# One Trainium2 core, a quantised decoder layer: x2's bias sums, integers and projections moved to other places

## The reference

```python
x = _layernorm(x + self_attention(x))                # q, k, v with bias, softmax, wo, bo
x = _layernorm(x + cross_attention(context, x))      # keys and values from the context
x = _layernorm(x + ffn(x))

def _qlinear(x, W, b):
    xq, sx, zx = _affine_quantize(x)                 # scale from max(x) - min(x) over the whole tensor
    wq, sw = _sym_quantize(W)
    return jnp.einsum('bsh,oh->bso', xq - zx, wq) * (sx * sw) + b
h = gelu(_qlinear(x, W1, b1)); out = _qlinear(h, W2, b2)      # 128 -> 512 -> 128
```

## Time and profile before

| | us |
|---|---|
| median of 3 runs | 332.87 (332.35 to 334.61) |
| the profiled execution, time | 331.59 |
| its span | 329.9 |
| busy: PE, DVE, ACT, POOL | 269.5, 299.9, 248.1, 238.6 |
| row maxima on DVE, 128 of them | 156.2 busy, 9.5 idle before them |
| last row maximum ends | 244.3 |
| last root of x2 ends | 258.1 |
| extremes of h end | 300.8 |
| last normalisation ends | 326.7 |

### The profile page before, as it was taken

One profiled execution on the slowest core, in us unless ns is written; L12 is line 12 of the kernel. 1 busy time (PEld: TensorE's weight loads), 2 busy tenths in 40 slices (PEclk: granted clock), 3 DMA queues, 4 the chain that ended last, 5 costly groups with the idle time before them and its releaser, 6 DMA issues.

```text
span 329.9 us, 12489 instructions
## 1 busy us (share of the span) xinstructions
PE 269.5 (82%) x4927; PEld 168.4 (51%) x4927; DVE 299.9 (91%) x695; ACT 248.1 (75%) x502; POOL 238.6 (72%) x477
## 2 busy tenths in 40 slices
PE   4677987999999999999999988898887655536991
PEld 3455654666656566665656655555554212112561
DVE  5668799899999999999999999999988779987994
ACT  2237776989988888888888878788775399912995
POOL 2866787897677878687786887776559228998394
PEclk9999999999999999999999999999999897557797
DMA  2353324143342423334243234322100000000025
GB/s 65 111 152 92 108 76 129 52 125 92 107 122 64 123 67 115 84 99 125 69 123 92 79 97 131 90 78 61 52 5 0 3 0 0 1 0 0 2 79 177
DMA packets 48993, 25.14 MB, mean 76 GB/s; under 512 B 6440, under 2 KB 48808, under 8 KB 48936
## 3 DMA queue, kind: packets, MB, share of 16 engines
q1 hardware_dynamic: 46072, 23.55, 24.6%
q10 hardware_dynamic: 2864, 0.80, 1.0%
HBM read 9.39 MB, written 2.10 MB: 35 GB/s over the span
## 4 chain that ended last, share of the span: by engine, by line
POOL 36%; DVE 29%; issue 13%; PE 10%; ACT 5%; SPq 3%; DMA 2%; POOLq 1%; DVEq 0%; ACTq 0%
DVE neg_max L1044 15%; POOL rstd L640 5%; SPq L472 3%; POOL arena_h L670 3%; POOL var_eps L633 2%; ACT arena_h L903 2%; DMA arena_h<-parts_sk 2%; POOL parts_cq L439 2%; POOL parts_ck L439 2%; PE ps L1298 2%; POOL parts_cq L437 2%; POOL parts_ck L437 2%; POOL x_bias L659 2%; DVE o_stats L1206 1%; POOL parts_sq L439 1%
## 5 line engine op out<-in xcount | busy, mean ns | idle before, releaser
L1044 DVE TENSOR_REDUCE neg_max<-ps 128x8 f32<-128x1024 f32 x128 | 156.2, 1220 | 9.5 <-PE ps L1298 9.3
L852 ACT ACTIVATE probs<-ps 128x1024 f32<-128x1024 f32 x64 | 65.5, 1024 | 21.8 <-PE ps L1305 21.8
L843 ACT ACTIVATE probs<-ps 128x1024 f32<-128x1024 f32 x64 | 65.6, 1025 | 15.7 <-PE ps L1305 11.8
L1298 PE MATMUL ps<-arena_h 31*128 31x128 f16 x1024 | 52.3, 220 | 20.4 <-DVE neg_max L1044 11.2
L1298 PEld LDWEIGHTS ps<-arena_h 31*128 31x128 f16 x1024 | 30.5, 94 | 54.9 <-DVE neg_max L1044 38.4
L1305 PE MATMUL ps<-arena_h 32*128 32x128 f16 x1024 | 51.2, 217 | 0.9 <-ACT probs L852 0.9
L1326 PE MATMUL ps<-probs,arena_q 128*32 128x128 f32 x1024 | 41.2, 279 | 1.4 <-ACT u_sb L868 1.4
L1326 PE MATMUL ps<-probs,arena_h 128*32 128x128 f32 x1024 | 41.3, 279 | 0.0
L633 POOL TENSOR_TENSOR var_eps<-mean_var,eps_col 128x1 f32<-128x1 f32 x64 | 12.3, 192 | 38.1 <-DVE mean_var L1026 38.1
L640 POOL TENSOR_TENSOR rstd<-var_eps,minus_half 128x1 f32<-128x1 f32 x64 | 35.3, 551 | 4.7
L1305 PEld LDWEIGHTS ps<-arena_h 32*128 32x128 f16 x1024 | 29.2, 92 | 2.0 <-ACT probs L852 1.5
(11 more groups left out here) (182 smaller groups left out, 657.7 us busy)
## 6 DMA issues: line engine op xcount, KB each, us to landing
arena_h<-parts_sq SPq DMA_DIRECT2D x48, 64.0 KB, 1.9
arena_h<-parts_ck SPq DMA_DIRECT2D x48, 64.0 KB, 2.3
arena_h<-parts_sk SPq DMA_DIRECT2D x46, 64.0 KB, 2.0
arena_h<-parts_cq SPq DMA_DIRECT2D x45, 64.0 KB, 2.2
xT_in<-in_xT_dram SPq DMA_DIRECT2D x16, 128.0 KB, 2.5
xN_in<-in_xN_dram SPq DMA_DIRECT2D x16, 128.0 KB, 2.6
cT_in<-in_cT_dram SPq DMA_DIRECT2D x16, 128.0 KB, 2.5
cN_in<-in_cN_dram SPq DMA_DIRECT2D x16, 128.0 KB, 2.3
```

The source lines that it names most:

```text
L843: act.activation(probs[1][:, :], ps_s2, ACT.Exp, scale=SCALE).then_inc(ex, 1)
L852: act.activation(probs[0][:, :], ps_s2, ACT.Exp, scale=SCALE).then_inc(ex, 1)
L1044: dve.tensor_reduce(neg_max[b.par][:, HH * half:HH * half + HH], ps_s1.rearrange("p (h k) -> p h k", h=HH), AXX, ALU.max, negate=True).the ...
L1298: ins = pe.matmul(ps_s1[:, at:at + S], q[r:r + MAX_AT, j, :], kk[r:r + MAX_AT, j, :], start=True, stop=True, skip_group_check=True)
```

## The change

Five things are moved; the arithmetic is the same.

1. **Ramp.** `LEAD_SLOTS` goes. A table `RAMP` gives each half of slots -2 to 2 at most one projection. Four buffers of `xT_in` in place of two, the third and fourth loaded at the start. k of pairs 0 to 2 goes to bank 4, v of pairs 1 and 2 to banks 2 and 3 (the banks of the shifted scores). GpSimd splits pair 3 a slot earlier, ahead of the block weights.
2. **Cross fill.** ScalarE issues the first cross q's two DMAs of the high part as soon as that is there; SP issues the third. The scaling of w2 (L700) goes from slot 7 to 8.
3. **Last exponentials.** The second half of the shifted scores of the last three tasks goes to `ps_s1`.
4. **x2 + b2.** The four sums go directly behind the last root on GpSimd, into a buffer of their own (the space of the x and split buffers, now one arena). GpSimd folds a fifth unit.
5. **Second stage.** GpSimd clips units 4 to 7 to integers, in front of the output roots. VectorE scales a fifth unit (9) itself. VectorE's statistics of groups 0 to 2 go between and behind the integers of the third chunk.

```diff
-DVE_ALONE = (1, 3, 5, 7)
+DVE_ALONE = (1, 3, 5, 7, 9)
-LOADS = 2
+LOADS, X_LOADS = 2, 4
-SCALE_AT, INTS_AT = (6, 7), (9, 10)
-LEAD_SLOTS = 2
+SCALE_AT, INTS_AT = (6, 8), (9, 10)
+RAMP = {(-2, 0): ("v", 1), (-2, 1): ("q", 2), (-1, 0): ("k", 2), (-1, 1): ("v", 2), (0, 0): ("q", 3),
+        (1, 0): ("k", 3), (1, 1): ("v", 3), (2, 0): ("q", 4), (2, 1): ("k", 4)}
-FOLDED_UNITS = (3, 6, 9, 12)
-EXTREMES_ORDER = (1, 2, 4, 5, 3, 7, 8, 6, 10, 11, 9, 13, 14, 12, 15)
+FOLDED_UNITS = (3, 6, 9, 11, 13)
+EXTREMES_ORDER = (1, 2, 4, 5, 3, 7, 8, 6, 10, 12, 9, 14, 11, 15, 13)
...
+        def shifted_bank(t, half):
+            return ps_s1 if half == 1 and t.pos >= TASKS - 3 else ps_s2
...
             def x2_bias(c):
-                t = x2_all[:, c * 8:(c + 1) * 8, :]
-                pool.tensor_tensor(t, t, b2_wide[:, :].unsqueeze(1).broadcast_to([128, 8, D]),
-                                   ALU.add).then_inc(f_b, 1)
+                if c == B // 8 - 1:
+                    pool.wait_ge(xn, made_to(C_POS[B - 1], False))
+                pool.tensor_tensor(arena_x[:, c * 8 * D:(c + 1) * 8 * D].rearrange("p (b d) -> p b d", d=D),
+                                   x2_all[:, c * 8:(c + 1) * 8, :],
+                                   b2_wide[:, :].unsqueeze(1).broadcast_to([128, 8, D]), ALU.add).then_inc(f_b, 1)
...
+            for c in range(B // 8):
+                x2_bias(c)
             x_ints(2)
             x_ints(3)
             fold_unit(0)
             x_ints(4)
-            fold_unit(1)
-            pool.wait_ge(f_xi, DVE_PIECES)
-            pool.wait_ge(f_xp, NP - DVE_PIECES)
-            x2_bias(0)
-            fold_unit(2)
-            x2_bias(1)
-            fold_unit(3)
-            x2_bias(2)
-            x2_bias(3)
+            for n in range(1, len(FOLDED_UNITS)):
+                fold_unit(n)
...
+            pool.wait_ge(f_lh, 1)
+            for u in (4, 6, 5, 7):
+                h_ints(u)
...
                 if 0 in cq_pairs(k):
                     act.wait_ge(c_cleared, 1)
-                    act.wait_ge(split_done["cq"], 1)
-                    for t, part in enumerate(Q_PARTS):
+                    act.wait_ge(split_hi["cq"], 1)
+                    for t in (0, 1):
...
+                    if name == "q":
+                        if i < 4:
+                            pe.wait_ge(eqk, 2 * i - 1)
+                        else:
+                            pe.wait_ge(evv, i)
+                        project_q(i)
+                    if name == "k":
+                        pe.wait_ge(eqk, 2 * i if i < 3 else 2 * i + 1)
+                        project_k(i)
```

More of the change, by code:

```diff
@@ L192, in xT_pairs @@
 def xT_pairs(k):
-    ahead = [(i, XT_AT if i < LEAD_PAIRS else XT_LATER_AT) for i in range(LOADS, PAIRS)]
+    ahead = [(i, XT_AT if i < LEAD_PAIRS else XT_LATER_AT) for i in range(X_LOADS, PAIRS)]
     return [i for i, at in ahead if S_POS[2 * i] - at == k]
@@ L250, in decoder_layer @@
         arena_q = sb("arena_q", [128, NHC * B * S // 2])
[L251 removed]
+        xT_in = [sb(f"xT_in{i}", [128, PAIR]) for i in range(X_LOADS)]
         cT_in = [sb(f"cT_in{i}", [128, PAIR]) for i in range(LOADS)]
@@ L673, in slot @@
                     last.then_inc(vc, 1)
-                i = S_FIRST.get(k + QK_AT)
-                if i:
+                i = 3 if k == 0 else S_FIRST.get(k + QK_AT)
+                if i and not (i == 3 and k != 0):
+                    if i == 3:
+                        blocks()
                     pool.wait_ge(eqk, 2 * i + 1)
@@ L803, in slot, with q_out @@
                 a, z, w, v, nxt = task(k), task(k - 1), task(k - 2), task(k - 6), task(k + 1)
-                def evacuations():
[L805 to L811, removed]
-                                           bias=bqk_sb[:, j:j + 1]).then_inc(eqk, 1)
+                def q_out(i):
+                    if i == 0:
+                        act.wait_ge(b_ready, 1)
+                    act.wait_ge(pqk, 2 * i + 2 if i == LEAD_PAIRS - 1 else 2 * i + 1)
+                    need(act, split_done["sq"], i)
+                    act.activation(q_full[:, :], q_sums(i), ACT.Identity, bias=bqk_sb[:, 0:1]).then_inc(eqk, 1)
@@ new lines, in k_out, with v_out @@
+                def k_out(i):
+                    act.wait_ge(pqk, 2 * i + 2)
+                    need(act, split_done["sk"], i)
+                    act.activation(k_full[:, :], k_sums(i), ACT.Identity, bias=bqk_sb[:, 1:2]).then_inc(eqk, 1)
+                def v_out(i):
+                    if i == 0:
+                        act.wait_ge(cleared, 1)
+                        act.wait_ge(split_hi["sk"], 1)
+                        for t in (0, 2):
+                            act.dma_start(stack["sk"][0][t::ROW_STEP, :, :],
+                                          parts["sk"][0][:, K_PARTS[t], :]).then_inc(stacks_landed("sk", 0)[0], 16)
+                        act.wait_ge(v0_ready, 2)
+                    elif i == 1:
+                        act.wait_ge(v_ready, 1)
+                    act.wait_ge(pvv, i + 1)
+                    if i >= RING:
+                        act.wait_ge(pv, 2 * S_POS[2 * (i - RING) + 1] + 2)
+                    src = v_sums(i).rearrange("p (b i j e) -> p b i j e", b=4, i=2, j=4)
+                    for col in range(2):
+                        last = act.copy(v_places(v_pair("S", i % RING), col, 16 * col, E), src[:, :, col, :, :])
+                    last.then_inc(evv, 1)
@@ L813, in evacuations, with ramp_out @@
+                def ramp_out(k, half):
+                    name, i = RAMP.get((k, half), (None, None))
+                    if name is not None:
+                        {"q": q_out, "k": k_out, "v": v_out}[name](i)
+                def evacuations():
+                    if q_pair(k) is not None:
+                        q_out(q_pair(k))
+                    if k_pair(k) is not None:
+                        k_out(k_pair(k))
                     i = S_FIRST.get(k + V_AT)
                     if i is not None:
[L815 to L824 removed]
@@ L1230, in _ @@
                 if half == 0:
-                    o_sums(NG - 4)
-                    o_sums(NG - 3)
-            o_sums(NG - 2)
-            o_sums(NG - 1)
+                    o_sums(3)
+            for g in range(4, NG):
+                o_sums(g)
             g = NG - 1
```

192 lines of the change are left out of this document (119 added, 73 removed).

## The result

| | before | changed |
|---|---|---|
| median, us | 332.98 (6 runs, 332.35 to 334.61) | 336.19 (6 runs, 335.33 to 336.56) |
| ratio to before | | 1.0092 (95%: 1.0071 to 1.0113) |
| profiled execution: span, us | 329.9 | 334.5 |
| last row maximum starts | 243.0 | 241.7 |
| last root of x2 ends | 258.10 | 256.86 |

The changed kernel is 3.1 us slower (2.4 to 3.8), where I forecast 0.6 faster, with a range up to 335.5 that it left. By the two traces, up to the last root it is 1.24 us shorter, from there to the extremes of h 3.3 longer, and the second stage 2.6 longer. That adds to 4.7, not 3.1, because the profiled execution of before lay 1.4 us under its own median; the part on the clearing of stacks says what is known of that.

The account below looks back on a forecast made before the run. VectorE was taken to bound attention and the second stage until the last root, TensorE close beside it there. Terms -3.9 + 1.6 + 1.7 = -0.6 us took 332.87 to 332.3 us; 8 in 10 range 325.5 to 335.5.

Parts of the forecast that it names:

- (a): Slot 2: pair 2 projected earlier, its k stack filled about 2 us earlier, VectorE's 0.99 us wait goes: -1.0 us.
- (g): Last exponentials: scores of the last three tasks lie under the exponential before, ScalarE waits less: -0.3 us.
- x2 + b2 behind the last root: Last root to extremes of h: VectorE waits for GpSimd's sums, a fifth fold saves some: +1.6 us.
- integers on GpSimd: Second stage: GpSimd's four integer units take turns with VectorE's words and integers: +1.7 us.
- The rivals without a bill: One bill not sent: 327.8 or 329.6 us, chance 0.22; neither bill sent: 325.1 us, chance 0.15.
- the one of the clock: Second stage: TensorE's clock falls to its lower level for at least three groups: some 337 us, chance 0.08.
- The rival that the ramp gives nothing: Attention: SP's queue or the new waits take (a) to (c) back: 334.8 us, chance 0.07.
- (c): Slot 6: q and k of pair 4 evacuated earlier, TensorE's 1.07 us stack wait goes: -1.0 us.
- (b): Slot 3: q or k of pair 4 no longer stands before the scores VectorE waits for: -0.5 us.
- (d): Slots -1 and 0: slot 0's first half freed, a slow-clock projection before both second halves: 0, bounds -0.6 and +0.6.
- (e): Cross fill: ScalarE issues two DMAs in place of three, VectorE's 1.46 us wait behind them shrinks: -0.8 us.
- (f): Slot 8: the scaling L700 no longer holds up a normalisation on VectorE: -0.3 us.

Follow-up runs that it names:

- e3: Changed kernel with the x2 + b2 sums back between GpSimd's folds and the second stage's integers back on VectorE; ratio 0.9951 to before, -1.6 us.
- e1: Changed kernel with the x2 + b2 sums back between GpSimd's folds, four folded units; ratio 1.0027 to before, +0.9 us.
- e2: Changed kernel with all second-stage integers back on VectorE, in the order of before; ratio 1.0023 to before, +0.8 us.
- e11: Changed kernel with ten products that nobody reads in place of four, where TensorE waits for the x integers; ratio 1.0084 to before.
- e4: Changed kernel with GpSimd clearing all four cross stacks before the first normalisation; ratio 1.0084 to before.
- e10: e3 with GpSimd clearing all four cross stacks before the first normalisation; ratio 0.9897 to before.
- e5: Kernel before with GpSimd clearing all four cross stacks before the first normalisation; ratio 0.9958 to before.
- e8: Changed kernel with e2's edit, sums in GpSimd's idle places, early clearing, and two third-chunk integer units on GpSimd after VectorE's second chunk; ratio 0.9927 to before.

## Why the prediction was wrong

| term | forecast | measured |
|---|---|---|
| attention, (a) to (g) | -3.9 | -1.6 (e3 against before: -1.0 to -2.3) |
| x2 + b2 behind the last root | +1.6 | +2.2 to +2.4 (e1, e3) |
| integers on GpSimd | +1.7 | +2.3 to +2.5 (e2, e3) |
| sum | -0.6 | +3.1 |

The case I held likeliest was the right mechanism: attention gains, both bills are sent. Three sizes were off, all on the same side, by 2.3, 0.7 and 0.7 us. Only the first is clear of the noise; 1.6 and 1.7 us lie within the intervals of the two bills. The rivals without a bill are refuted by e1 and e2, the one of the clock by e11's trace of the second stage. The rival that the ramp gives nothing is not refuted by a time: (a) to (c) were 2.5 of my 3.9 us, so by it attention would give 1.4, and e3 measures 1.6. No run undoes the ramp alone. What speaks against it is the traces, where the maxima of slot 6 start 0.8 to 2.4 us earlier than before in all eleven kernels with the new ramp.

**Attention, the largest miss.** The step that failed is the sum of (a) to (g): I took each wait in front of a maximum as winnable by itself, and asked only of SP and TensorE what comes next. By the starts of the maxima, after against before, single traces both:

- (a), (b) and (d) together give 0.9 us by slot 3, forecast 1.5. The waits of slots 2 and 3 did shrink, but slot 1 has new ones. (d) looked at slots -1 and 0 and put the projections there at 0; that of k of pair 3 in slot 1 stands in no term. It takes 0.95 or 1.06 us in four of the eleven traces with this ramp (changed, e1, e4, e11), and the gain by slot 3 is then 0.1 to 0.9; in the other seven it takes 0.60 to 0.77, and the gain is 1.0 to 1.6. What makes it longer in some is open.
- (c) gives 1.0 in the first half of slot 6, as forecast, of which 0.5 goes back in the second, to the maximum of 1.69 us.
- (e) and (f) give 0.6 of 1.1 by slot 11; the wait behind the cross fill is 0.86 where I took 1.46 - 0.8.
- Slot 12 gives 0.75 back, to the maximum of 2.02 us.
- (g) gives nothing: the last exponentials save 0.15, and the copy behind them waits 0.97 for TensorE in place of 0.79.

So in this pair of traces 1.3 us of the 2.7 that are missing go to VectorE's own normalisation, held by clearing instructions. They stood in the trace of before (44.44 for 1.36 us, 68.26 for 1.71), and I had counted them only among the 16 that "take longer than 0.4 us". Three of these waited past a second instruction of GpSimd, not two.

The times put less on the clearing. In e10 against e5, both without clearing there, the same edits are worth 2.0 us, with about 1.3 on either side, against 1.6 with it. So some 1.9 of my 3.9 were missing even so. In those two traces (a), (b) and (d) give 1.2 us, (c) 0.3, since e5 has most of that stack wait gone already, and (e) and (f) 0.5 by slot 12; behind it they drift another 1.0 us apart, which no term explains. How the miss splits between the terms stays rough: in changed, e1, e2 and e3, whose attention part is the same, the last maximum starts at 241.74, 243.31, 240.80 and 241.80.

**The sums.** The waits were where I put them up to the second sum. After that I had VectorE meet GpSimd only at the x integers; it met it three times on the way, for 0.25 us at a 2x2 step and for 1.08 and 1.53 at steps with two SBUF inputs, as the Trainium skill (GPSIMD Engine Reference, Key points) has it. I priced the latter at 0.6 us beside the sum and left it out of the forecast. First extreme against last root: 5.4 us later than before, forecast 4.7. The fifth fold saved less than reckoned, since folds and gelus still made VectorE wait 1.9 us (1.0 forecast). Together that is 3.3 by the traces in place of 1.6; the times say 2.2 to 2.4. There was also a slip in the sum: begin at 270.3, 31.3 of work and 1.0 of waiting end at 302.6, not at 302.3, so my own terms gave +1.9.

**The integers.** First statistics 10.4 us behind the scales in place of 6.8: +3.5, forecast +3.4. VectorE's last aggregate: +1.7 against the scales, as forecast. What failed is the step behind it, "the last root and L1244 follow", which put nothing on GpSimd. GpSimd had become the late engine, with 11.8 us of roots for seven groups, and added 1.1 us: the wait of 0.99 became 2.05. e8 shows the same limit from another side.

## What to carry to other kernels

In these runs work on GpSimd cost VectorE nothing beside its statistics and its row reductions, but held up its SBUF-to-SBUF TENSOR_SCALARs and its steps with two SBUF inputs. A tiny VectorE step on the path can wait out a whole GpSimd instruction, so cut such instructions to fit a gap and let the last end before the step is ready. When an edit makes one engine earlier, list what is queued next on every engine at the new time, clearing and folding included; and look at several executions before a wait of the trace is priced: here the same attention code ended 2.5 us apart in two of them.

## What was not expected of the hardware

- In the profile an instruction behind a waiting one on VectorE starts before the wait is over: at 43.93 and 66.65 the maximum's duration is 1.69 and 2.02 us in place of 1.22, ending at the same moment as the normalisation. So a normalisation of 2.12 us cost the queue 0.47.
- A normalisation can wait past five clearing instructions in a row (2.12 and 2.45 us), in other executions past two (1.36 and 1.71).
- Size does not decide the wait: a 2x2 TENSOR_SCALAR took 2.30 us and a 128x1 TENSOR_TENSOR 1.68. Other steps of the same chain did not wait. VectorE beside the fourth sum, changed kernel:

```profile
263.81 0.17 DVE L1197 RECIPROCAL quant<-quant 128x1 f32<-128x1 f32 x1
264.01 0.22 DVE L1205 TENSOR_SCALAR quant<-ps,quant 128x1 f32<-128x1 f32 x1
264.14 0.14 DVE L1206 TENSOR_SCALAR quant<-quant 128x1 f32<-128x1 f32 x1
264.32 0.15 DVE L1208 TENSOR_SCALAR quant<-quant 128x1 f32<-128x1 f32 x1
```

The TENSOR_SCALARs from SBUF to SBUF that waited have 2, 128 or 1024 elements per partition; the two here that did not (264.14, 264.32) have one. But these two also take constants as their second operand, and those that waited take values from SBUF. Which of the two decides is left open.
